# Attention of a four-stage transformer: F32R parts in 32-row groups for stacked bf16 parts, one maximum row, mask in VectorE's maximum, unrolled

## What is computed

```python
x = _layernorm(x + _L0_attn_ref(x, Wqkv, Wproj))        # causal attention, 16 heads of 8, output projection
x = _layernorm(x + _L0_ffn_ref(x, ln_g, ln_b, Wr, ...)) # mixture of experts, top 2 of 7, one shared
x = _layernorm(x + _L1_attn_ref(x, Wq, Wk, Wv))         # attention without mask, 16 heads of 8, no projection
x = _layernorm(x + _L1_ffn_ref(x, w1_w, ...))           # dense layers, ternary weights
```

```python
Q = _apply_rope(Q, cos, sin); K = _apply_rope(K, cos, sin)
scores = einsum('bhqd,bhkd->bhqk', Q, K) / sqrt(8)      # L0: where(causal, scores, lowest)
y = einsum('bhqk,bhkd->bhqd', softmax(scores), V)
```

## Time and profile before

| | us |
|---|---|
| median of 3 runs | 1817.08 |
| profiled execution, span | 1812.5 |
| TensorE busy (matmuls) | 1304.5 |
| VectorE busy | 977.7 |
| ScalarE busy | 856.7 |
| GpSimd busy | 521.3 |
| mean granted TensorE clock, share of full | 0.842 |

### The profile page before, as it was taken

The page is one execution under the profiler, slowest core; times in us unless marked ns, Lnnn a source line. Parts: engine busy times, 40 slices in busy tenths (PEclk is TensorE's granted clock), DMA queues, the critical chain, the costliest instruction groups (busy, mean ns, idle before and its releaser), DMA issues. The chain is left out here.

```text
span 1812.5 us, 26221 instructions
## 1 busy us (share of the span) xinstructions
PE 1304.5 (72%) x7355; PEld 675.7 (37%) x7355; DVE 977.7 (54%) x2508; ACT 856.7 (47%) x1575; POOL 521.3 (29%) x452
## 2 busy tenths in 40 slices
PE   1657648576595868784195876969678696899997
PEld 0323324233242355562021222213122122688885
DVE  2536446364374569345284855758467583235353
ACT  1235335253363574443143644647455475455553
POOL 6213133131241256473520201102021100345453
PEclk7669678697797969897567987989788799899999
DMA  4343241332422030342543314132240400000000
GB/s 72 38 55 35 33 54 29 51 37 31 54 38 30 2 119 0 93 82 61 58 88 38 39 22 53 20 47 29 31 49 16 49 2 7 12 12 15 20 12 18
DMA packets 84625, 70.22 MB, mean 39 GB/s; under 512 B 7628, under 2 KB 78476, under 8 KB 84508
## 3 DMA queue, kind: packets, MB, share of 16 engines
q1 hardware_dynamic: 80060, 64.78, 23.5%
q0 software_dynamic: 4176, 3.55, 1.4%
q10 hardware_dynamic: 272, 0.52, 0.1%
HBM read 17.84 MB, written 8.06 MB: 14 GB/s over the span
## 5 line engine op out<-in xcount | busy, mean ns | idle before, releaser
L671 DVE TENSOR_REDUCE a_mx<-a_ps_m 128x1 f32<-128x512 f32 (+3 forms) x864 | 547.2, 664 | 458.3 <-PE a_ps_m L535 254.2
L436 ACT ACTIVATE a_prob<-a_ps_s 128x512 f32<-128x512 f32 (+1 forms) x864 | 468.8, 576 | 505.7 <-PE a_ps_s L548 503.1
L548 PE MATMUL a_ps_s<-a_qst,a_kst 96*128 96x512 bf16 (+3 forms) x1024 | 349.3, 371 | 209.5 <-DMA a_qst<-a_mrow 172.0
L532 PE MATMUL a_ps_m<-a_kst,a_qst 72*128 72x512 bf16 (+3 forms) x1024 | 359.7, 376 | 152.5 <-DMA a_qst<-a_part_q 141.6
L548 PEld LDWEIGHTS a_ps_s<-a_qst,a_kst 96*128 96x128 bf16 x1024 | 93.1, 101 | 502.8 <-issue 246.6
L564 PE MATMUL a_ps_o<-a_prob,a_vst 128*32 128x512 f32 (+3 forms) x2048 | 245.4, 554 | 0.3 <-POOL a_prob L392 0.3
L392 POOL TENSOR_SCALAR_AFFINE_SELECT a_prob<-a_prob 128x512 f32<-128x512 f32 x128 | 81.2, 634 | 426.0 <-ACT a_prob L436 426.0
L532 PEld LDWEIGHTS a_ps_m<-a_kst,a_qst 72*128 72x128 bf16 x1024 | 107.5, 105 | 216.6 <-issue 172.2
L355 POOL TENSOR_TENSOR a_turned_k<-a_turned_k,sin_table 128x512 f32<-128x512 f32 x14 | 17.7, 1262 | 419.6 <-DVE a_rope_k L644 419.4
L1782 POOL TENSOR_TENSOR f_hid_lo<-f_gelu_h,f_hid_hi 128x512 fp32r<-128x512 f32 x64 | 83.1, 1298 | 101.0 <-ACT f_hid_hi L1745 101.0
L535 PE MATMUL a_ps_m<-mask,identb 128*128 128x128 bf16 x512 | 111.0, 240 | 0.0
(11 more groups left out here) (312 smaller groups left out, 1993.4 us busy)
## 6 DMA issues: line engine op xcount, KB each, us to landing
a_kst<-a_part_k SPq DMA_DIRECT2D x144, 128.0 KB
a_qst<-a_part_q SPq DMA_DIRECT2D x138, 128.0 KB
f_w<-in_L_ffn_W_dram SPq DMA_DIRECT2D x21, 256.0 KB, 3.6
a_xin<-in_L_attn_x_dram SPq DMA_DIRECT2D x8, 256.0 KB, 2.8
x_tiles<-in_L_attn_x_dram SPq DMA_DIRECT2D x8, 256.0 KB, 3.1
normed_rows_dram<-f_nrm SPq DMA_DIRECT2D x8, 256.0 KB, 2.3
f_hT_hi<-expert_sums_dram SPq DMA_DIRECT2D x4, 512.0 KB, 5.7
a_xin<-x_tiles SPq DMA_DIRECT2D x8, 256.0 KB, 2.4
```

Of the source, the lines that this page charges most:

```text
L436: act.activation(prob[j % RING][:, h:h + nu, 0:w], ps_s[(g * SU + u0 + slot) % SBANKS][:, 0:nu * w] .rearrange("p (h t) -> p h t", h=nu), ...
L532: last = pe.matmul(bank[:, v * w:v * w + w], qst[r][0:ROWS, h, P * i:P * i + P], kst[r][0:ROWS, h, 0:w], start=True, stop=not causal)
L548: last = pe.matmul(pbank[:, v * w:v * w + w], kst[r][:, h, P * j:P * j + P], qst[r][:, h, T - w:T], start=True, stop=True)
L671: dve.reduce_max(mx[:, g % 2, i, u * mh:u * mh + mh], ps_m[(unit + g * MU) % MBANKS][:, 0:mh * w] .rearrange("p (h t) -> p h t", h=mh), AX.X)\
```

## The change

`attention` is rewritten; the work in each stage around it stays.

- **Two F32R parts a head.** q and k are split into hi and lo of F32R. A head takes 24 rows (k: lo, hi, hi; q: hi, hi, lo) and one more for the maximum: 25 rows in a group of 32 (`QUAD`). The four heads of a group lie in the four 32-row groups of the array; `kst` and `qst` are [128, 4, 512] F32R. SP copies hi twice and lo once for each of the four row groups, for k and for q: 24 copies of [8 partitions x 4 x 512] a batch.
- **One maximum row**, rounded to F32R, for three; VectorE no longer splits it. Ones lie in `kst` from a memset.
- **The mask** of the maxima is added in VectorE: `tensor_tensor_reduce` of the bank and a row tile `maskw` takes the place of `reduce_max` and of the mask matmuls. GpSimd still zeroes the diagonal of `prob`.
- **Banks**: scores 3, maxima 2, small jobs 2 (before 2, 4 and 1), one for the values.
- **Units**: each holds one head. The causal attention has 12 of them a group (512; 384 + 128; 256 columns).
- **Order**: maxima unit u belongs to head (u + 2) mod 4, so scores and maxima that stand together are in different row groups. k, q, v are made two batches ahead (v one), k and q are read out of PSUM by ScalarE, and the rotation lies on GpSimd.
- **Unrolled**: no loops in `attention`; one set of semaphores for both calls, cleared at the start of `moe_ffn`.

The core of the diff:

```diff
-                    for row in stack_rows(m):
-                        sp.dma_start(dst[row:row + D, :, :], part[name][:, part_no, :]).then_inc(s_st[name], 16)
...
+                def stack(b):
+                    r = b % 2
+                    if b >= 2:
+                        sp.wait_ge(s_score, (b - 1) * NG * U)
+                    for name, dst, s_dst, hi_rows, lo_rows in (("k", kst[r], s_kst[r], (D, 2 * D), (0,)),
+                                                               ("q", qst[r], s_qst[r], (0, D), (2 * D,))):
+                        sp.wait_ge(s_hi[name], b + 1)
+                        for i in range(HG):
+                            for row in hi_rows:
+                                sp.dma_start(dst[QUAD * i + row:QUAD * i + row + D, :, :].bitcast(F32),
+                                             hi[name][QUAD * i:QUAD * i + QUAD, :].bitcast(F32)).then_inc(s_dst, 16)
+                        sp.wait_ge(s_lo[name], b + 1)
...
+                for n in range(G):
+                    if n + 1 < G:
+                        max_row(n + 1)
+                    if n % NG == 0 and n // NG + 1 < B:
+                        stack(n // NG + 1)
...
+                def scores(n, u):
...
+                    if u == 0:
+                        pe.wait_ge(s_mst, (n + 1) * 16)
+                    after(pe, s_exp, g - SB + 1)
+                    lo_row, end = QUAD * i, QUAD * i + KROWS + 1
+                    for j, col, w in sh.score[k]:
+                        last = pe.matmul(ps_s[g % SB][:, col:col + w], kst[r][lo_row:end, t, P * j:P * j + P],
+                                         qst[r][lo_row:end, t, T - w:T], start=True, stop=True)
...
+                def maxima(n, u):
...
+                    if u == 0 and t == 0:
+                        pe.wait_ge(s_kst[r], stacked(b))
+                        pe.wait_ge(s_qst[r], stacked(b))
+                    i = (i + 2) % HG
+                    after(pe, s_mx, g - MB + 1)
...
+                for n in range(G):
+                    for u in range(U):
+                        scores(n, u)
+                        if n + 2 < G:
+                            maxima(n + 2, u)
+                        for back, j in sh.values.get(u, []):
+                            if n >= back:
+                                values(n - back, j)
+                        for name, m in sh.jobs(n, u):
+                            job(name, m)
...
+                        if causal:
+                            ins = dve.tensor_tensor_reduce(junk[g % MB][:, col:col + w], bank[:, col:col + w], maskw[:, T - w:T], 1.0, -3.0e38,
+                                                           ALU.add, ALU.max, out)
+                        else:
+                            ins = dve.reduce_max(out, bank[:, col:col + w], AX.X)
```

More of the change, by code:

```diff
@@ L20 @@
 PARTS = 3
[L21 to L24, removed]
+QUAD = 32
+KROWS = 3 * D
+SWAP = [(i + QUAD // 2) % QUAD for i in range(QUAD)]
 VW = 32
@@ L135, in scale_steps @@
     return 2 * tiles + 5 + 3 * NEWTON
[L138 to L151, removed]
-    G = B * NG
[L153 to L199, removed]
@@ L201, in attention @@
+def attention(nc, sems, x, x_dram, ident, maskw, weights, wproj, cos, sin, tag, ahead=None):
+    causal = maskw is not None
+    sh = Shapes(causal)
+    U = sh.units
+    G = B * NG
+    SB, MB, XB = 3, 2, 2
+    START = [("xT", 0), ("k", 0), ("q", 0), ("v", 0), ("xT", 1), ("k", 1), ("q", 1), ("maxT", 0)]
+    END = [("norm", G - 1)] + ([("yT", B - 1), ("proj", B - 1)] if causal else [])
+    place = sh.ring(START, END, XB)
     with ExitStack() as ctx:
@@ L396, in _ @@
-                batch(0, 0, first=True)
-                with pool.Fori(0, B // 2 - 1) as it:
-                    batch(2 * it + 1, 1)
-                    batch(2 * it + 2, 0)
-                batch(B - 1, 1, last=True)
+                for r in range(2):
+                    pool.memset(kst[r][:, :, :].bitcast(F32), 1.0).then_inc(s_ones, 1)
+                for step in range(5):
+                    rope(pool, 0, "k", step)
+                for name in "kq":
+                    for step in range(5):
+                        rope(pool, 1, name, step)
@@ L486, in _, with job @@
+                out_read(G - 1)
+                if causal:
+                    read_out("yT", B - 1)
             @block.tensor
             def _(pe):
-                def job(name, b, r, n, count, bank=ps_x):
-                    pe.wait_ge(s_job_free, n + 1 if bank is ps_x else FREED)
+                def job(name, n):
+                    slot, before = place[name, n]
+                    ps_x = ps_j[slot]
+                    if before is not None:
+                        pe.wait_ge(s_read[before[0]], before[1] + 1)
@@ L615, in _ @@
-                pe.wait_ge(s_vinit, 4)
-                batch(0, 0, first=True)
-                pe.wait_ge(s_ones, 32)
-                with pe.Fori(0, B // 2 - 1) as it:
-                    batch(2 * it + 1, 1)
-                    batch(2 * it + 2, 0)
-                batch(B - 1, 1, last=True)
-                for j in range(QT - LAG, QT):
-                    values(B - 1, 1, NG - 1, j)
-                n = jobs_before(B - 1, False) + len(batch_jobs(False, True))
-                job("norm", None, None, n, G - 1)
@@ L626, in _ @@
-                if wproj is not None:
-                    job("yT", B - 1, 1, n + 1, None)
-                    job("proj", B - 1, 1, n + 2, None)
+                        after(pe, s_oT, n)
+                        if t == 0:
+                            pe.wait_ge(s_read["v"], b + 1)
+                    for i in range(HG):
+                        last = pe.matmul(ps_o[VW * i:VW * i + VW, T - w:T], vst[b % 2][:, j, HG * t + i, :],
+                                         prob[k][:, i, col:col + w], start=(j == 0), stop=(j == sh.order[-1]))
```

804 lines of the change are left out of this document (357 added, 447 removed).

## The result

The changed kernel takes **1741.22 us** (median of 4 runs, 1737.11 to 1744.65), the kernel before 1815.49 us on the same chip: a ratio of 0.9589 (95% interval 0.9563 to 0.9614). It is faster by 74 us where 265 were forecast, and the time lies outside the forecast's range of 1390 to 1670 us. The mean granted clock of TensorE fell from 0.842 to 0.684.

The account below looks back on a forecast made before the run. Stack copies setting the time while engines idle bound the kernel; savings of 139 us causal, 121 us second attention and 5 us starts cut the span from 1812.5 to 1547.5, median 1552 us; 8-in-10 range 1390 to 1670.

Parts of the forecast that it names:

- A copy: One 64 KB stack copy in either attention, priced by bytes at the old 60 GB/s: 1.09 us.
- S: Time for a batch's 24 stack copies in either attention: 26.2 us.
- The first rival: Stack copies not held by their narrow destination: 15.4 us a batch, attention waits nearly vanish, 1395 us; chance 0.12.
- the third: Rival: each stack copy costs 2.18 us whatever it holds, 52.3 us a batch, 1970 us; chance 0.04.
- The stall: TensorE's wait at the third group for the maximum row behind the copies: some 10 us a batch causal, 4 second.
- a + S + 1.5 + 3 + 2 P: Batch period: lead a (3.8, 3.0 us), S, row landing, low-clock restart, two groups P; 54.5 us causal, 60.1 second.
- P: Length of one attention group, paced by VectorE: 10.0 us causal, 13.2 us in the second attention.
- The second rival: Longer attention groups at TensorE's low clock: 13 us causal, 17 second, 1678 us; chance 0.14, drains included.
- The drain: Tiling-mode changes drain TensorE in attention: 2.3 us a group, 83 us over 36 groups, 1635 us; within a 0.14 chance.
- Row groups side by side: Attention scores and maxima in different 32-row groups run two at once; without overlap, time near 1560 us.
- The second piece of the maximum: Small second VectorE operation behind each causal masked maximum: taken as 0.1 us each, 0 to 3.2 us a group possible.

Follow-up runs that it names:

- run 4: Changed kernel with each of the 24 stack copies issued a second time to a spare tile, both waited for: 2121.6 us (one execution).
- run 1: Changed kernel with the maxima taking the same head and 32-row group as the scores beside them, so none overlap: 1948.2 us, ratio to before 1.072.
- run 5: Changed kernel with scores and maxima reading all 128 rows, summed over four heads (computation changed), no overlap possible: 1563.3 us, ratio to before 0.863.
- run 3: Changed kernel with three PSUM banks for the maxima and one for small jobs, instead of two and two: 1619.6 us, ratio 0.893.
- run 12: Changed kernel with banks 3, 3, 1, third causal key tile, two heads per 64-row half with zero-filled queries, maxima opposite scores: 1489.3 us, ratio to before 0.811.
- run 13: As run 12, but the maxima take the same half of the rows as the scores, so no two matmuls overlap: 1583.8 and 1630.2 us (two executions).
- run 9: Changed kernel with matmuls over 96 or 97 rows, one zero-filled query tile per head, banks 2, 3, 2: 1553.1 us, ratio to before 0.857.

## Why the prediction was wrong, by its own steps

**What bounded the kernel before** was read rightly: the copies. They moved in 39 us a batch and take 21 to 25 now.

**A copy** was put at 1.09 us by bytes. In batches of 24 it measured 0.86 to 1.03 us, and SP needs 0.74 us to issue one, so S is 21 to 25 and not 26.2 us. In run 4's batches of 48 it is 0.96 to 1.13 us: so bytes at the old rate are a fair price there, and somewhat too high a one for 24. The first rival's 0.64 us was not reached, and the third (2.18 us whatever it holds) is out. The fixed 2 us of the Trainium skill, "SBUF — State Buffer", The DMA setup-cost knee, did not add up over the copies of a queue. By the Trainium skill, "SBUF — State Buffer", Door 1, the estimate was 54.4 GB/s; run 4's 57 GB/s is near it, and the changed kernel's batches are above it (1.57 MB in 20.6 us are 76 GB/s, in 25 us 63).

**The stall** was to stay, at 10 and 4 us a batch. It went almost entirely (6.5 us in all), because a group was no longer 10.0 and 13.2 us. The period formula a + S + 1.5 + 3 + 2 P holds only while the copies outlast two groups. Otherwise a period is 4 P, and that is what the trace has: 4 x 13.95 = 55.8 for the 54.5 forecast, where two errors cancelled (a longer group, no stall), so that this part came near by luck; and 4 x 19.7 = 78.9 for 60.1. (By the formula as it stands the first rival's causal period is 43.7 us and not 42, and its time 1407.)

**The step that failed is P,** and in it one sentence: "Against it: scores, maxima and values together would fill PE at the low level, as they do before the clock rises now". They did fill PE, 43.26 of 44 us, and the clock stayed at 0.51. In its place stands a clock of 0.61 and 0.58 in the attentions, and a P of 13.9 and 19.6 us for 10.0 and 13.2. I had taken the clock for something that being busy earns. The kernel before had its maxima and scores over 72 and 96 rows, at 1.00; the change put 24 and 25 in their place. It was written in the diff, and in the prediction it only counted as a chance for overlap. Run 1 shows busy without clock, run 5 clock with rows.

**The second rival** was the right one, and was undersized: 13 and 17 us a group, for 13.9 and 19.6 measured. A term was missing. The ring of two maxima banks was priced with a matmul of 0.38 us ("barely keeps up"); with one of 0.79 it is 0.79 us a unit, and a third bank alone gives 122 us and groups of 13.6 and 16.2 us (run 3), though with a clock of 0.67 in the second attention.

**The drain,** which the same rival held, does not show as a price of the row pieces. The Trainium skill, "TensorEngine Tiling (Array Packing)", Key Properties, has a change of mode drain the engine. From the last 512-column matmul to the value product behind it, the medians at the low clock are 0.72 us in the changed kernel, but 0.55 in run 1, which changes between 25 rows and the whole array too, and 0.56 in run 5, which stays at 128 rows. At the full clock they are 0.42 us in run 12 and 0.33 in runs 13 and 5. So the longer step goes with the pair that overlaps before it, and not with the change from row pieces. The way back, from the value product to the next score, takes 0.52 us at the full clock in runs 5, 12 and 13 alike. All of these runs go from 128 to 32 columns and back, so they cannot show whether that change costs something.

**Row groups side by side:** as forecast, 3 to 10 ns apart; without it the change would have been 7% slower than the kernel before (run 1, 1948 us), where the prediction had put a change without overlap near 1560, by the full clock again.

**VectorE** does not pace the changed kernel. The second piece of the maximum, put at 0.1 us, costs about 0.01. With the clock up, run 12 has groups of 13.5 us in the second attention, near the 13.2 that were worked out for VectorE, and run 5 the forecast's kind of stall (48.5 us for the maximum row).

**The end** was left out. Behind the last transposed maxima ScalarE reads the last output 34.5 us later (1445.83 - 1411.31), before 21.0 us later (1521.98 - 1500.94): 13.5 of the 15.4 us at the end, with the clock at 0.55 for 1.00.

## What to carry to other kernels

Ask of a packed matmul how many rows of the array it keeps at work, and not only what it costs alone: cutting a product into small row groups can leave the clock at its lower level however busy TensorE is (0.50 in run 1), and there the columns take twice as long. Filling rows with zeros costs no columns; two halves of the array side by side had both the overlap and the clock (run 12). A stall that a formula keeps should be checked against the new length of what covers it, since a period is the longer of two sums; and a ring of banks must be sized for the slow clock too.

## What the runs showed that I had not expected

- The clock stood at 0.50 for both attentions while PE was busy for 90% of the time with matmuls of 24 and 25 rows (run 1), and at 1.00 with 128 rows in the same order (run 5). The Trainium skill, "TensorE: Matmul & The Clock Gate", Part 1, lets the clock be set by how busy TensorE has been lately, and has idle gaps bring it down; by that, run 1 should have been at the higher level, and the measurement says otherwise.
- Rows that hold zeros on the side of the queries bring the clock up as well: 0.98 in the second attention with some 24 of 97 rows filled (run 9), 0.99 where all 128 are read (run 5).
- One kernel can have both levels in the same work, 60 us at 1.00 and 83 us at 0.50 (run 13), and its two executions differ by 3%.
- The change between row pieces and the whole array cost nothing that can be seen: 0.55 us with it (run 1), 0.56 without (run 5).
- The read of a maximum with a fused mask, 83 ns, lies beside the next operation and costs some 0.01 us.
